# Decoder layer, cross-attention output: stored as half-precision pairs and brought back by transposing DMAs, with one copy less in the running maximum

## Chip, cores, metric

One Trainium2 chip, one core. The metric is device microseconds of one execution; lower is better. TensorE is called PE here, VectorE DVE, ScalarE ACT, GpSimd POOL, and SP is the engine whose queue issues all DMAs of this kernel.

## What is computed

One post-norm decoder layer over 16 sequences of 112 tokens (1792 tokens, width 256): grouped self-attention, then cross-attention, then a feed-forward network with ternary weights, each followed by `layernorm(x + f(x))`. The part that takes most of the time is the cross-attention. All 1792 queries attend to all 16 x 375 = 6000 context rows, in 8 heads of 128:

```
qh, kh, vh = split_heads(x @ Wq), split_heads(ctx @ Wk), split_heads(ctx @ Wv)   # [8, 1792|6000, 128]
sim  = (qh @ kh.T) * 128**-0.5
mean = sim.mean(-1);  sim = (sim - mean) * 1.5 + mean        # a shift per query, which softmax ignores
out  = softmax(sim) @ vh                                      # [8, 1792, 128] -> [1792, 1024]
y    = out @ Wout + bout                                      # [1792, 256]
x    = layernorm(x + y)
x    = layernorm(x + gelu(x @ T(W1).T + b1) @ T(W2).T + b2)   # T: ternary
```

All products keep single-precision accuracy by splitting each operand into a high and a low half-precision part (`f16`) and adding three of the four products.

## The kernel before

**Stages.** Self-attention takes the first 190 us or so. Cross-attention follows, and then a tail with output projection, second layernorm, feed-forward network and third layernorm.

**Cross-attention.** The work is 56 blocks: head h (8) by block of 256 queries (7), `n = 7 h + qb`. The 6016 padded keys of a block are 12 groups of 4 tiles of 128 keys (the last group has 3 tiles). A group is numbered `f = 12 n + s`, 672 in all. At step (n, s) each engine does, in an order written out by hand, a piece of several groups at once:

- PE computes the scores of group f+17 (`scores`, 12 matmuls of 128x256 into a pair of PSUM banks that alternate with f), then `attend(f)`: exponentials, high and low, times the values, added up over the block in bank 4 or 5. Between them lies a `side` task, one that prepares keys, values or queries of a later block. At s = 8 comes `spread`, which writes the row maxima of the next block over all partitions into bank 6.
- ACT copies the scores of group f+17 out of PSUM to a ring of 16 slots in single precision (`keep_scores`, line 847). It waits there until POOL has done with the group that held the slot. It computes the exponentials of group f+3 (`exp_half` for even groups, `exp_full`, lines 854 and 862).
- DVE takes the running maximum of group f+17 straight from PSUM into `run_max` (f16): for the first group of a block a plain copy (line 1081), for the other eleven a maximum with what is in `run_max` (line 1084). PE's `scores` may overwrite a pair of banks when that has been done. DVE also subtracts the maximum from group f+4 (line 1105). At s = 6 it folds the block's maximum (`fold_max`, line 1091). SP transposes the folded maximum with a DMA (`turn`, line 1691), and at s = 8 DVE reduces it (`rows_max`, line 1098); `spread` and the first subtraction of the next block wait for that.
- POOL casts the exponentials of odd groups to f16 (line 1622) and computes the low parts of all groups (line 1628) up to group 658 (`LATE`); after that the low parts of odd groups are DVE's (`low_weights`, line 1124).

**The output of a block.** At s = 1 of the following block DVE inverts the two sums (`invert_sums`) and ACT writes both query tiles, scaled, as single-precision numbers into `o_buf` (`store_output`, 128x128 each). At s = 2 DVE adds a remaining product to the first one (`add_low`, line 1117), and SP stores `o_buf` to DRAM (`store`, line 1680).

**Output projection.** The 1792 rows are 14 tiles of 128 tokens. For each tile SP loads [128 tokens x 1024] in single precision (`load_tile`, 512 KB, line 1699) into one of 5 buffers. PE transposes it in 8 matmuls of 128x128 into banks 0 and 1 (`o_transposes`, line 673). ACT copies the high part out (`o_high`, line 966), DVE computes the low part (`o_low`, line 1311), and PE projects it with 24 matmuls of 128x256 (`o_project`, line 693). Tiles 0 to 4 are transposed at steps TAIL, TAIL+3, ... (TAIL = 657 is step 9 of block 54). Tiles 0 to 3 are projected three steps later each, in three portions after `attend`, the others after the last block, between the pieces of the feed-forward network (`up`, `down`) and its transposes (`n_transposes`).

**SP's queue** is one list in order. What matters near the end is this (block 53 is h = 7, qb = 4):

```
store(53)                       # waits for add_low of block 53, which DVE does in block 54
load_tile(0), (1), (2)
turn(55)                        # the folded maximum of the last block, made at s = 6 of block 54
load of res2                    # the residual stream, 1792 KB
load_tile(3), (4), (5)          # after POOL is through group 657
store(54); load_tile(6) .. (9)
store(55); load_tile(10) .. (13)
```

A `load_tile` waits until the stores of its rows have landed and until its buffer is free.

Of the kernel before, what the change touches and what calls it, by code (L numbers as in the profile page):

```python
# [5 lines left out]
F32 = mybir.dt.float32  # L6
F16 = mybir.dt.float16
ALU = mybir.AluOpType
# [63 lines left out]
def build(nc, xT, x, WA, Wo, ctxT, Wq, Wk, Wv, Wout, bout, W1T, b1, W2T, b2, o_dram, out):  # L72


    with ExitStack() as top:
# [7 lines left out]
        def sem(name):  # L83
# [39 lines left out]
        raw = [at(o, f"raw{r}", [P, NH, DH], F32)  # L123
               for r, o in enumerate((VREG, VREG + 4096, WREG, RING, RING + 4096))]
# [3 lines left out]
        t_dram = nc.dram_tensor("t_scratch", (4, P, W12), F16, kind="Internal").ap()  # L128

        res = at(RING + 12 * 4096, "res", [T, NB, D], F32)  # L130
        res2 = at(KREG, "res2", [P, NT // P, D], F32)
        o_part = o_dram[:, 0:INNER]
# [101 lines left out]
        def batch_tokens(b, n=T):  # L234
# [20 lines left out]
        o_buf = at(SMALL + 32, "o_buf", [P, QT, DH], F32)  # L255
# [10 lines left out]
        (s_qk, s_kept, s_max, s_sub, s_hi, s_exp, s_cast, s_lo, s_av, s_fold, s_bc, s_den, s_oev, s_olo, s_od,  # L266
         s_init) = [
            sem("b_" + n) for n in ("qk", "kept", "max", "sub", "hi", "exp", "cast", "lo", "av", "fold",
                                    "bc", "den", "oev", "olo", "od", "init")]
# [9 lines left out]
        def cols_of(s):  # L279
            return tiles_of(s) * QB  # L280

# [58 lines left out]

        TAIL = NF_ALL - 15
        O_TURN = {3 * i: i for i in range(5)}
        BIASED = {6 + 2 * i: i for i in range(5)}
        O_PROJECT = {3 * i + 3 + x: (i, range(*w)) for i in range(4) for x, w in enumerate(((0, 3), (3, 6), (6, 8)))}
# [9 lines left out]
        oT_hi = [at(KREG + 14336 + 2048 * r, f"oT_hi{r}", [P, NH, P], F16) for r in range(2)]  # L354
        oT_lo = [at(KREG + 18432 + 2048 * r, f"oT_lo{r}", [P, NH, P], F16) for r in range(2)]
# [12 lines left out]
        def bank_of_projection(p):  # L368
            return (7, 3, 2)[p] if p < 3 else 6

        def bank_of_output(p):
            return 6 if p == 5 else 7
# [21 lines left out]
        def columns(c):  # L394
# [7 lines left out]
        (t_bias, t_tr, t_hi, t_lo, t_wp, t_n, t_cp, t_n3, t_add, t_nt, t_yh, t_yl, t_f1, t_ge, t_hh, t_hl, t_f2, t_add2,  # L402
         t_bn, t_bn2, t_ag, t_sq, t_ag3, t_sq3, t_shift,
         t_n3a, t_last, t_out) = [
            sem("t_" + n) for n in ("bias", "tr", "hi", "lo", "wp", "n", "cp", "n3", "add", "nt", "yh", "yl", "f1", "ge",
# [3 lines left out]
        with nc.Block() as block:  # L409

            @block.tensor
            def _(pe):
                def scores(f, more, more_sides, s, qpar):

                    if f >= 2:
                        pe.wait_ge(s_max, more + (f - 1))
# [247 lines left out]
                def o_transposes(i):  # L664
                    pe.wait_ge(s_raw[i % NRAW], 16 * (i // NRAW + 1))
                    if i:
                        pe.wait_ge(t_lo, i)
                    else:

                        pe.wait_ge(s_max, NF_ALL)  # L670
                        pe.wait_ge(s_ident2, 2)
                    for h in range(NH):
                        mm = pe.transpose(psum[:, h // 4, (h % 4) * P:(h % 4 + 1) * P], raw[i % NRAW][:, h, :],
                                          ident2[:, :])
                    mm.then_inc(t_tr, 1)

                def o_project(i, heads=range(NH)):
                    p = i // 2
                    if heads[0] == 0:
                        pe.wait_ge(t_lo, i + 1)  # L680
                        if i == 0:

                            pe.wait_ge(s_free, len(SIDES))
                            pe.wait_ge(s_late, 48)
                        elif i == 6:

                            pe.wait_ge(s_sub, NF_ALL)
                        elif i % 2 == 0 and p >= 4:

                            pe.wait_ge(t_add, p)  # L690
                    for h in heads:
                        for n, (o, w) in enumerate(((oT_hi, wout_hi), (oT_hi, wout_lo), (oT_lo, wout_hi))):
                            mm = pe.matmul(psum[:, bank_of_projection(p), (i % 2) * D:(i % 2 + 1) * D],  # L693
                                           lhsT=o[i % 2][:, h, :], rhs=w[:, h, :],
# [1090 lines left out]
```

## Time and profile before

| | |
|---|---|
| median of 3 runs | 2296.75 us (2296.54 to 2297.69) |
| the profiled execution's own time | 2296.72 us |
| its span in the trace | 2294.9 us |
| busy: PE / DVE / ACT / POOL | 2239.2 / 1972.6 / 1862.2 / 1897.7 us |
| granted clock of PE, mean | 0.998 |
| chain that ended last | PE 83%, POOL 6%, DVE 5%, ACT 2%, issue 2%, DMA 1% |

The span is the stretch between the first and the last recorded instruction; 1.82 us of the execution's time lie around it. Busy times are sums over an engine's instructions; PE's matmuls overlap, so its share says that it was never without one, not that it ran at its peak. Times in the views are microseconds from the start of the span. An entry such as "[1.61 <-DMA ...]" says that the engine stood idle for 1.61 us before the instruction, and what ended that.

### The profile page before, as it was taken

The numbers are of one execution on the slowest core, as the hardware profiler recorded it, in microseconds if no ns is written. First come the engines' busy times: TensorE is split into PE (matmuls) and PEld (weight loads), VectorE is DVE, ScalarE is ACT, GpSimd is POOL, SyncE is SP. The second block draws the span as 40 slices with busy tenths as digits, with TensorE's granted clock in tenths as the row PEclk, the third lists the DMA queues.
The fourth block names the chain that finished last, engine by engine and source line by source line (L and its number), as shares of the span: only waits on it lengthen the run. The fifth ranks groups of instructions, "written<-read, shape, count | busy, mean of one in ns | idle before, by whom it ended". The sixth has DMA issues, their size and how long they took to land.

```text
span 2294.9 us, 61829 instructions
## 1 busy us (share of the span) xinstructions
PE 2239.2 (98%) x25966; PEld 1972.6 (86%) x25966; DVE 1972.6 (86%) x2185; ACT 1862.2 (81%) x2224; POOL 1897.7 (83%) x1155
## 2 busy tenths in 40 slices
PE   7998999999999999999999999999999999999898
PEld 4557998899889998899888998899889988989886
DVE  7888888888888888888888888888888888888877
ACT  4457888888888888888878888888888888888855
POOL 8675888888888888888888898888888888899853
PEclk9999999999999999999999999999999999999999
DMA  6400000000000000000000000000000000011220
GB/s 200 159 32 26 9 9 15 9 11 9 16 9 9 11 8 16 9 9 11 15 9 9 9 9 15 11 9 9 15 9 11 7 11 9 9 24 36 96 79 33
DMA packets 65302, 57.77 MB, mean 25 GB/s; under 512 B 32769, under 2 KB 57857, under 8 KB 65025
## 3 DMA queue, kind: packets, MB, share of 16 engines
q1 hardware_dynamic: 65024, 53.81, 8.5%
q8 instruction: 207, 3.39, 0.6%
q14 instruction: 71, 0.57, 0.1%
HBM read 30.99 MB, written 15.47 MB: 20 GB/s over the span
## 4 chain that ended last, share of the span: by engine, by line
PE 83%; POOL 6%; DVE 5%; issue 2%; ACT 2%; DMA 1%; POOLq 0%; DVEq 0%; ACTq 0%
PE psum L426 32%; PE psum L458 11%; PE psum L451 11%; PE psum L456 6%; PE psum L454 6%; POOL e_lo L1628 5%; PE psum L573 4%; PE psum L563 4%; DVE run_max L1084 2%; PE psum L693 2%; PE psum L580 1%; POOL e_hi L1622 1%; DMA fold_t<-fold 1%; ACT ring L847 1%; PE psum L741 1%
## 5 line engine op out<-in xcount | busy, mean ns | idle before, releaser
L1628 POOL TENSOR_TENSOR e_lo<-ring,e_hi 128x1024 f16<-128x1024 f32 (+1 forms) x665 | 1387.5, 2101 | 195.1 <-ACT ring L862 165.1
L1084 DVE TENSOR_TENSOR run_max<-psum,run_max 128x1024 f16<-128x1024 f32 (+1 forms) x616 | 738.7, 1199 | 180.3 <-ACT ring L847 175.7
L847 ACT ACTIVATE ring<-psum 128x1024 f32<-128x1024 f32 (+1 forms) x672 | 673.7, 1003 | 169.0 <-PE psum L426 91.2
L1105 DVE SCALAR_TENSOR_TENSOR ring<-ring,psum 128x1024 f32<-128x1024 f32 (+1 forms) x672 | 793.8, 1188 | 0.4 <-PE psum L659 0.4
L426 PE MATMUL psum<-qx_hi,k_hi 128*128 128x256 f16 x2632 | 717.5, 273 | 7.8 <-DVE run_max L1084 7.8
L426 PE MATMUL psum<-qx_hi,k_lo 128*128 128x256 f16 x2632 | 717.3, 273 | 0.0
L426 PE MATMUL psum<-qx_lo,k_hi 128*128 128x256 f16 x2632 | 717.3, 273 | 0.0
L458 PE MATMUL psum<-v_main,e_lo 128*128 128x129 f16 x4032 | 710.8, 219 | 0.0
L862 ACT ACTIVATE ring<-ring 128x1024 f32<-128x1024 f32 (+1 forms) x672 | 696.3, 1037 | 0.9 <-DVE ring L1105 0.4
L451 PE MATMUL psum<-v_main,e_hi 128*128 128x257 f16 x2016 | 550.0, 273 | 3.0 <-POOL e_lo L1628 3.0
L456 PE MATMUL psum<-v_main,e_hi 128*128 128x128 f16 x2016 | 446.7, 222 | 0.0
L454 PE MATMUL psum<-v_main,e_hi 128*128 128x129 f16 x2016 | 445.5, 221 | 0.0
L854 ACT ACTIVATE e_hi<-ring 128x1024 f16<-128x1024 f32 x336 | 353.7, 1053 | 101.6 <-DVE ring L1105 101.6
L1622 POOL CAST e_hi<-ring 128x1024 f16<-128x1024 f32 x336 | 341.0, 1015 | 104.0 <-ACT ring L862 101.5
L458 PEld LDWEIGHTS psum<-v_main,e_lo 128*128 128x128 f16 x4032 | 395.5, 98 | 6.9
L426 PEld LDWEIGHTS psum<-qx_hi,k_hi 128*128 128x128 f16 x2632 | 256.8, 98 | 37.7 <-DVE run_max L1084 8.1
L426 PEld LDWEIGHTS psum<-qx_hi,k_lo 128*128 128x128 f16 x2632 | 257.4, 98 | 30.1
L426 PEld LDWEIGHTS psum<-qx_lo,k_hi 128*128 128x128 f16 x2632 | 257.4, 98 | 28.0
L454 PEld LDWEIGHTS psum<-v_main,e_hi 128*128 128x128 f16 x2016 | 197.3, 98 | 25.1
L458 PE MATMUL psum<-v_tail,e_lo 128*128 128x129 f16 (+1 forms) x1232 | 217.9, 219 | 0.0
L451 PEld LDWEIGHTS psum<-v_main,e_hi 128*128 128x128 f16 x2016 | 194.0, 96 | 10.4 <-POOL e_lo L1628 1.9
L456 PEld LDWEIGHTS psum<-v_main,e_hi 128*128 128x128 f16 x2016 | 197.6, 98 | 0.0
(202 smaller groups left out, 3090.2 us busy)
## 6 DMA issues: line engine op xcount, KB each, us to landing
o_scratch<-o_buf SPq DMA_DIRECT2D x56, 128.0 KB, 1.9
raw<-o_scratch SPq DMA_DIRECT2D x14, 512.0 KB, 4.4
stage<-in_ctxT SPq DMA_DIRECT2D x6, 500.0 KB, 4.1
stage<-in_ctxT SPq DMA_DIRECT2D x12, 250.0 KB, 4.9
w_scratch<-wall SPq DMA_DIRECT2D x1, 2304.0 KB, 11.0
wall<-w_scratch SPq DMA_DIRECT2D x6, 384.0 KB, 3.2
x<-in_xT SPq DMA_DIRECT2D x4, 448.0 KB, 6.1
res<-in_x SPq DMA_DIRECT2D x1, 1792.0 KB, 15.4
```

What stands on the lines that cost most here:

```text
L426: mm = pe.matmul(psum[:, 2 * (f % 2) + i // 2, (i % 2) * QB:(i % 2 + 1) * QB], lhsT=k[:, keys], rhs=q[:, qpar, :], start=(n == 0), stop=(n ...
L451: pe.matmul(psum[:, 4 + n % 2, 0:VW], lhsT=e_hi_f[keys, cols], rhs=v_f[keys, i, :], start=(s == 0 and i == 0), stop=False)
L454: pe.matmul(out_t, lhsT=e_hi_f[keys, cols], rhs=v_f[keys, i, 0:OW], start=False, stop=False)
L456: pe.matmul(out_t[:, 0:DH], lhsT=e_hi_f[keys, cols], rhs=v_f[keys, i, OW:VW], start=False, stop=False)
L458: mm = pe.matmul(out_t, lhsT=e_lo_f[keys, cols], rhs=v_f[keys, i, 0:OW], start=False, stop=last_tile and t == QT - 1)
L847: a.activation(ring[:, f % SLOTS, 0:n], pair(f)[:, 0:n], ACT.Copy).then_inc(s_kept, 1)
L854: a.activation(e_hi[f % NEH][:, 0:n], ring[:, f % SLOTS, 0:n], ACT.Exp, scale=SIM_SCALE).then_inc(s_hi, 1)
L862: a.activation(slot, slot, ACT.Exp, scale=SIM_SCALE).then_inc(s_exp, 1)
L1084: ins = v.tensor_tensor(run_max[:, 0:n], pair(f)[:, 0:n], run_max[:, 0:n], ALU.max)
L1105: v.scalar_tensor_tensor(slot, slot, LIFT, psum[:, 6, 0:QB].unsqueeze(1).broadcast_to([P, t, QB]), ALU.add, ALU.subtract).then_inc(s_sub, 1)
L1622: g.tensor_copy(e_hi[f % NEH][:, 0:n], slot).then_inc(s_cast, 1)
L1628: g.tensor_tensor(e_lo[f % NEL][:, 0:n], slot, e_hi[f % NEH][:, 0:n], ALU.subtract).then_inc(s_lo, 1)
```

## The change

Three things change.

1. The running maximum of a block's first group is not taken any more. The second group's maximum reads its own scores from PSUM and the first group's from the ring, in single precision. The copy of line 1081 goes; PE's wait before the scores that overwrite the first group's banks is now for ACT's copy to the ring.
2. The output leaves PSUM as f16 pairs. ACT writes the first query tile in single precision to `o_first` and the second tile's high part straight to `o_buf`. At s = 2 DVE adds the remaining product to `o_first`, computes the second tile's low part from PSUM, and casts `o_first` to its high part (`first_high`). At s = 3 it computes the first tile's low part (`first_low`). The store moves behind that, to s = 3. It has the same number of bytes, in another DRAM tensor whose row holds high and low part of each head. `fold_max` has one more wait, for the low part two blocks back.
3. `load_tile` becomes a transposing DMA [128 tokens x 2048] to [128, 8 heads, 2 parts, 128 tokens] of f16, 512 KB as before. There are 7 buffers. PE's transposes, `o_high` and `o_low` go, for all 14 tiles. Tile i of the first five is projected at steps TAIL+3i to TAIL+3i+2, so that five tiles instead of four are projected beside the last blocks, each from the step at which it was transposed before. After the last block each projection stands one place further ahead in PE's list. The projections rotate over other banks, and the first two `first_residual` of DVE run at TAIL+9 and TAIL+14.

```diff
 def scores(f, past, more_sides, s, qpar):
-    if f >= 2:
-        pe.wait_ge(s_max, more + (f - 1))
+    if f >= 2 and (f - 2) % NGRP == 0:
+        pe.wait_ge(s_kept, past * NQB * NGRP + (f - 1))
+    elif f >= 2:
+        pe.wait_ge(s_max, past * NQB * (NGRP - 1) + maxima_before(f - 2))
...
-            if s == 0:
-                ins = v.tensor_copy(run_max[:, :], pair(f))
-            else:
-                ins = v.tensor_tensor(run_max[:, 0:n], pair(f)[:, 0:n], run_max[:, 0:n], ALU.max)
+            if s == 1:
+                before = ring[:, (f - 1) % SLOTS, :]
+            else:
+                before = run_max[:, 0:n]
+            v.tensor_tensor(run_max[:, 0:n], pair(f)[:, 0:n], before, ALU.max).then_inc(s_max, 1)
...
 def store_output(n):
-    for t in range(QT):
-        a.activation(o_buf[:, t, :], psum[:, 4 + n % 2, O_AT[t]:O_AT[t] + DH], ACT.Copy,
+    for t, dst in enumerate((o_first[:, :], o_buf[:, 1, 0, :])):
+        a.activation(dst, psum[:, 4 + n % 2, O_AT[t]:O_AT[t] + DH], ACT.Copy,
                      scale=o_den[:, t:t + 1]).then_inc(s_oev, 1)
...
 def add_low(n):
     v.wait_ge(s_oev, n * QT + QT)
-    v.scalar_tensor_tensor(o_buf[:, 0, :], psum[:, 4 + n % 2, OW:VW], o_den[:, 0:1], o_buf[:, 0, :],
-                           ALU.mult, ALU.add).then_inc(s_olo, 1)
+    v.scalar_tensor_tensor(o_first[:, :], bank[:, OW:VW], o_den[:, 0:1], o_first[:, :],
+                           ALU.mult, ALU.add).then_inc(s_whole, 1)
+    v.scalar_tensor_tensor(o_buf[:, 1, 1, :], bank[:, O_AT[1]:O_AT[1] + DH], o_den[:, 1:2],
+                           o_buf[:, 1, 0, :], ALU.mult, ALU.subtract).then_inc(s_whole, 1)
+
+def first_high(n):
+    v.wait_ge(s_whole, 2 * n + 1)
+    v.tensor_copy(o_buf[:, 0, 0, :], o_first[:, :]).then_inc(s_ohi, 1)
+
+def first_low(n):
+    v.wait_ge(s_ohi, n + 1)
+    v.wait_ge(s_whole, 2 * n + 2)
+    v.tensor_tensor(o_buf[:, 0, 1, :], o_first[:, :], o_buf[:, 0, 0, :], ALU.subtract).then_inc(s_olo, 1)
...
-O_TURN = {3 * i: i for i in range(5)}
-O_PROJECT = {3 * i + 3 + x: (i, range(*w)) for i in range(4) for x, w in enumerate(((0, 3), (3, 6), (6, 8)))}
+O_PROJECT = {3 * i + x: (i, range(*w)) for i in range(5) for x, w in enumerate(((0, 3), (3, 6), (6, 8)))}
+RESIDUAL = {9: 0, 14: 1}
...
 def o_project(i, heads=range(NH)):
     if heads[0] == 0:
-        pe.wait_ge(t_lo, i + 1)
+        pe.wait_ge(s_raw[i % NRAW], 16 * (i // NRAW + 1))
...
-                   lhsT=o[i % 2][:, h, :], rhs=w[:, h, :],
+                   lhsT=raw[i % NRAW][:, h, o, :], rhs=w[:, h, :],
...
 # PE's list after the last block, without the removed o_transposes
-    o_project(4); n_transposes(0); o_project(5); n_transposes(1); o_project(6)
-    c=0: up, o_project(7), up, (8), down(0), n_transposes(2), (9), down(1), n_transposes(3), (10)
-    c=1: up, (11), up, (12), down(2), n_transposes(4), (13), down(3) in two halves with n_transposes(5) between
+    o_project(5); n_transposes(0); o_project(6); n_transposes(1); o_project(7)
+    c=0: up, o_project(8), up, (9), down(0), n_transposes(2), (10), down(1), n_transposes(3), (11)
+    c=1: up, (12), up, (13), down(2), n_transposes(4), down(3) in two halves with n_transposes(5) between
...
 def load_tile(i):
     sp.wait_ge(s_od, (NBLK - NQB + i // QT + 1) * 16)
     if i >= NRAW:
-        sp.wait_ge(t_tr, i - NRAW + 1)
-    sp.dma_start(raw[i % NRAW][:, :, :].rearrange("p h d -> p (h d)"),
-                 o_part[i * P:(i + 1) * P, :]).then_inc(s_raw[i % NRAW], 16)
+        sp.wait_ge(t_wp, i - NRAW + 1)
+    sp.dma_start_transpose(raw[i % NRAW][:, :, :, :].rearrange("p h x t -> p (h x) t"),
+                           halves_dram[i * P:(i + 1) * P, :]).then_inc(s_raw[i % NRAW], 16)
```

## Rows read from the trace of the kernel before

**Rows 1.** Windows: stretch, length, each engine's busy time, granted clock, DMA share, GB/s.
```profile
265.00:2000.00 1735.00, 1722.99 (x20454) 1563.10 (x20452) 1511.49 (x1559) 1490.10 (x1750) 1489.79 (x865) 1.00 0.05 10
2000.00:2171.00 171.00, 161.53 (x1929) 148.61 (x1927) 149.28 (x147) 147.21 (x167) 156.89 (x94) 1.00 0.16 46
2171.00:2201.00 30.00, 29.98 (x364) 28.33 (x365) 24.70 (x25) 18.77 (x22) 25.67 (x22) 1.00 0.33 110
2201.00:2266.20 65.20, 65.01 (x530) 52.63 (x529) 48.14 (x102) 35.26 (x52) 22.35 (x30) 1.00 0.13 43
```

**Rows 2.** Waits of PE, 265 to 2000: total, times, longest.
```profile
PE psum L659 <- DVE row_max L1098: 6.2, 10, 1.2
```

**Rows 3.** Instructions by tile: ns min/median/max, first and last start.
```profile
L673 PE MATMUL psum<-ident,raw x112: 272/273/303, 2166.1 to 2252.7; 128*128 128x128 f32 x112
...
L966 ACT ACTIVATE oT_hi<-psum x14: 999/1023/1027, 2168.6 to 2253.0; 128x1024 f16<-128x1024 f32 x14
L1311 DVE TENSOR_TENSOR oT_lo<-psum,oT_hi x14: 1210/1218/1226, 2169.6 to 2254.6; 128x1024 f16<-128x1024 f32 x14
...
L1081 DVE CAST run_max<-psum x56: 1210/1224/1226, 158.2 to 2128.6; 128x1024 f16<-128x1024 f32 x56
```

**Rows 4.** The chain that ended last, stretch 2150 to 2295: start, us, what.
```profile
2173.52 0.87 PE psum L673 x8
...
2201.98 2.62 PE psum L693 x24
...
2262.23 0.70 DVE res L1319
...
2263.75 0.26 DVE mean L1328 x2
...
2265.48 0.61 DVE yT_lo L1348
```

**Rows 5.** Waits of PE, 2160 to 2201.
```profile
PE psum L451 <- POOL e_lo L1628: 2.6, 2, 1.4
PE psum L659 <- DVE row_max L1098: 1.9, 1, 1.9
```

**Rows 6.** Timeline of SP's queue: start, us, instruction.
```profile
2150.31 0.36 SPq L1680 DMA_DIRECT2D o_scratch<-o_buf  x1
2150.77 2.40 SPq L1699 DMA_DIRECT2D raw<-o_scratch  x3
2161.41 1.20 SPq L1691 DMA_TRANSPOSE fold_t<-fold  x1
```

**Rows 7.** Timeline of DVE at the last folded maximum.
```profile
2163.86 0.69 DVE L1098 TENSOR_REDUCE row_max<-fold_t 128x2 f16<-128x512 f16 x1 [1.61 <-DMA fold_t<-fold]
```

**Rows 8.** DMA issues of the page: KB each, median us to landing.
```profile
fold_t<-fold SPq DMA_TRANSPOSE x56, 2.4
```

**Rows 9.** Windows over one transposing DMA of 128 KB, issued at 1235.58.
```profile
1236.50:1237.00 0.50, 0.50 (x11) 0.47 (x8) 0.00 (x0) 0.50 (x1) 0.47 (x1) 1.00 0.43 86
1237.00:1237.50 0.50, 0.50 (x11) 0.49 (x10) 0.12 (x1) 0.50 (x2) 0.50 (x1) 1.00 0.88 176
```

**Rows 10.** Timelines of DVE and POOL around 1196, and all folds by line.
```profile
1196.31 1.30 DVE L1091 TENSOR_TENSOR fold<-run_max 128x512 f16<-128x512 f16 x1
...
1196.29 1.04 POOL L1622 CAST e_hi<-ring 128x1024 f16<-128x1024 f32 x1 [0.61 <-ACT ring L862]
...
L1091 DVE TENSOR_TENSOR fold<-run_max x56: 415/419/1301, 189.7 to 2160.3; 128x512 f16<-128x512 f16 x56
```

**Rows 11.** Timelines of DVE, POOL and ACT in a block of the last head.
```profile
2049.39 0.34 DVE L1117 SCALAR_TENSOR_TENSOR o_buf<-psum,o_den,o_buf 128x128 f32<-128x128 f32 x1
...
2052.19 1.21 DVE L1105 SCALAR_TENSOR_TENSOR ring<-ring,psum 128x1024 f32<-128x1024 f32 x1
...
2050.34 4.24 POOL L1628 TENSOR_TENSOR e_lo<-ring,e_hi 128x1024 f16<-128x1024 f32 x2
...
2054.43 1.05 ACT L854 ACTIVATE e_hi<-ring 128x1024 f16<-128x1024 f32 x1
```

More of the change, by code:

```diff
@@ L121, in build @@
         wpack = [wall[:, i, :, :] for i in range(2)]
-        raw = [at(o, f"raw{r}", [P, NH, DH], F32)
-               for r, o in enumerate((VREG, VREG + 4096, WREG, RING, RING + 4096))]
+        raw = [at(o, f"raw{r}", [P, NH, 2, P], F16)
+               for r, o in enumerate((VREG, VREG + 4096, WREG, RING, RING + 4096, KREG + 14336, KREG + 18432))]
         NRAW = len(raw)
@@ L754, in step @@
                     if target < NBLK:
-                        scores(n * NGRP + ahead, past * NQB * NGRP, past * HEAD_SIDES, ts, target % 2)
+                        scores(n * NGRP + ahead, past, past * HEAD_SIDES, ts, target % 2)
                     task = side_of(n, s)
@@ L1024, in _ @@
                         roots(3)
-                    if f - TAIL in O_TURN:
-                        o_high(O_TURN[f - TAIL])
                 store_output(NBLK - 1)
@@ L1401, in last_norms, with first_residual @@
                                         ALU.subtract, ALU.mult).then_inc(t_last, 1)
+                def first_residual(p):
+                    of = res2[:, 2 * p:2 * p + 2, :]
+                    v.wait_ge(t_bias, 2 * p + 2)
+                    v.wait_ge(t_wp, 2 * p + 2)
+                    v.scalar_tensor_tensor(of, psum[:, bank_of_projection(p), :].rearrange("p (i d) -> p i d", i=2),
+                                           1 / WSCALE, of, ALU.mult, ALU.add).then_inc(t_add, 1)
+                    v.wait_ge(t_add, p + 1)
+                    for i in (2 * p, 2 * p + 1):
+                        v.bn_stats(bn2[:, i, :], res2[:, i, :]).then_inc(t_bn, 1)
                 self_attention()
@@ L1422, in _ @@
                         low_half(n, s, halves)
-                    if f + LEAD < NF_ALL:
+                    if f + LEAD < NF_ALL and (f + LEAD) % NGRP:
                         running_max(f + LEAD)
@@ L1431, in _ @@
                         add_low(n - 1)
+                        first_high(n - 1)
+                    if s == 3 and n > 0:
+                        first_low(n - 1)
                     if s == MAX_S and n + 1 < NBLK:
@@ L1440, in _ @@
                             inverse(3)
-                    if f - TAIL - 1 in O_TURN:
-                        o_low(O_TURN[f - TAIL - 1])
-                first_residual(0)
+                    if f - TAIL in RESIDUAL:
+                        first_residual(RESIDUAL[f - TAIL])
                 invert_sums(NBLK - 1)
-                first_residual(1)
                 add_low(NBLK - 1)
+                first_high(NBLK - 1)
+                first_low(NBLK - 1)
                 second_statistics(0)
-                o_low(5)
                 second_norms(0)
-                o_low(6)
                 n_low(0)
                 first_residual(2)
-                o_low(7)
                 n_low(1)
                 hidden_low(0, range(0, 4))
-                o_low(8)
                 first_residual(3)
@@ L1474, in _ @@
                 hidden_low(1, range(4, 8))
-                o_low(13)
                 second_norms(2)
```

120 lines of the change are left out of this document (37 added, 83 removed).

## The prediction

> **What bounds the kernel.** I read the windows first. From 265 to 2000 PE is busy for 1723.0 of 1735.0 us at full clock [rows 1], and what it waits for there is small: 6.2 us for the row maxima [rows 2]. DVE is busy for 87% of that stretch. So an instruction taken off DVE, ACT or POOL there gives time back only where PE waits for it. From 2000 on, in the last head, PE has few side tasks. POOL is busy for 156.9 of 171 us, and PE stands for 9.5 us [rows 1]. From 2171 to 2266 PE is full again: 29.98 of 30.00, then 65.01 of 65.20 [rows 1]. That last stretch is where the change has something to take. The chain of waits agrees: after 2171 it is PE's matmuls, with eight transposes of 0.87 us for each output tile among them, until two dependent chains of small operations near the end [rows 4]. Just before 2171 PE waits 1.9 us for the row maxima of the last block and 2.6 us for low parts from POOL [rows 5]. The row maxima came that late because DVE waited 1.61 us for the transposing DMA of the last folded maximum [rows 7].
>
> **Transposes on PE (gain).** There are 14 x 8 of them [rows 3]. 8 take 0.87 us, 0.109 each at PE's pace [rows 4]. Those of tile 0, at 2166, lie in front of an idle stretch of PE and cost nothing. The other 13 lie on the full stretch: 13 x 0.87 = 11.3 us. ACT's `o_high` (14 x 1.02) and DVE's `o_low` (14 x 1.22) [rows 3] run beside that, and I cost their removal at nothing. PE stays the bound there: two steps take it about 2 x 2.33 = 4.7 us (1.35 for `attend`, 0.98 for nine matmuls of a projection), and POOL's cast, low part and bias, 1.04 [rows 10], 2.12 [rows 11] and 0.7, make 3.9.
>
> **Tile 0's projection (gain).** Its 24 matmuls take 2.62 us [rows 4]. They start three steps earlier, at 2166, where PE has the 0.87 of the transposes and 1.4 of waiting for POOL [rows 5], 2.3 in all. If the row maxima come later still (below), all 2.6 is hidden. I take 2.6.
>
> **New waits of PE (loss).** With less between them, two dependent chains show. After the last `attend`, PE has 0.66 + 2.62 us of projections before `n_transposes(0)`. That needs the normalised tiles 0 and 1, behind: the reciprocal 0.2, ACT's two copies 0.7, two DVE operations of 0.34 [rows 11], the new cast and subtraction at some 0.2 each (a third to a half of that row's size, an estimate), and statistics to norms, which took 1.7 at the end (2263.75 to the low part) [rows 4]. With hand-overs that is about 4.1. So PE waits 0.8. The second is before `up(2)`. It needs `n_low(5)`, in DVE's list behind `first_residual(6)`, 3.9 us of chain (2262.23 to 2266.09) [rows 4]. The 24 matmuls of tile 13 stood between and now stand ahead of `down(2)`. From the end of `down(2)` PE has 40 matmuls, 4.4 us, and DVE's chain is 2.3 (transposes, residual, low part of pair 4) + 3.9 = 6.2. It waited some 0.2 before: 1.6 more. Together 2.4.
>
> **The loads (loss).** This is the term I know least. `turn(55)` stands in SP's queue behind loads 0 to 2. Before, these were issued in 2.40 us from 2150.77, long before 2161.41, when the folded maximum was ready [rows 6]. Now the store of block 53 comes one step later (`first_low` at s = 3), so loads start at about 2153.6, 7.8 us ahead of `turn(55)`. Let r be the time per transposing load, for issue or for transfer, whichever is longer. The last row maxima are then late by D = 3r - 7.8, if positive. The wait for them is on the path already [rows 5, 7], and POOL, ACT and PE follow at once, so D is lost in full. For r the trace shows no such load, but one of a quarter of the size from SBUF: SP is held for 1.20 us [rows 6], the DMA engines are busy for some 0.65 us (0.43 and 0.88 of two half microseconds) [rows 9], the landing takes 2.4 [rows 8]. Lower bound: four times the busy time, r = 2.6, D = 0. Upper bound: four times the landing, r = 9.6, D = 21. Nearest is SP's time, as it is issue that blocks the queue. A plain load holds SP for 0.3 to 0.8; if that much of 1.20 is fixed and the rest goes with size, r = 3.6, D = 3.0. I take 3.0. Loads 3 to 13 have room: with r up to 6 each lands before its projection.
>
> A rule of the Trainium skill speaks for the lower bound: "Advanced Engine Details and Errata", section X-Bar Transpose (TRN2), says that transposing DMAs are as fast as regular ones, 350 to 400 GB/s. By that a load is 1.5 us and D is 0. The windows show 86 and 176 GB/s for the small one [rows 9], so I don't rest on it. Another speaks against the change: "VectorE: DVE Perf Modes", section The three transpose paths, gives 1.3 us for one 128x128 block by DMA and 0.39 by TensorE; 16 blocks would be 21 us a load and the sum a loss. Four blocks landed in 2.4 us here [rows 8], so that figure doesn't simply add up.
>
> **Running maximum (nothing).** The copy, 56 x 1.22 us [rows 3], goes from DVE. It stood at s = 7, between the fold and the row maxima. Where PE waits for those, DVE was waiting for the DMA at the time [rows 7], so the copy hid in that wait. Lower bound of the price 0, best case the 6.2 us [rows 2]. The reading of the ring in single precision beside PSUM I cost like the copy's 1.22, as both rates go by PSUM.
>
> **Output in halves (loss, small).** Each block gets three more DVE operations: 0.34, and twice about 0.2. In sum that is less than the copy that goes, but they stand elsewhere, at s = 2 and 3. Two read SBUF alone, and such an operation waits for POOL: the fold, 0.42 at the median, took 1.30 when POOL's cast began 0.02 us before it [rows 10]. In the last head POOL works without a gap from 2050.34 to 2054.58 [rows 11]. `first_low` would come at about 2052.7, just where the second of the two instructions has begun, and would wait up to 2.0. The subtraction that ended at 2053.40 would then end near 2056.1 instead, and ACT, which needed it at 2054.43 [rows 11], would be 1.7 late, POOL 1.2. POOL is the bound there: 1.2 x 6 blocks = 7.2 us. Had it come 0.1 us earlier, it would slip in between the two and cost POOL 0.2, or 1.2 us. I take 2.0 in all, nearer to the small end, since DVE's phase to POOL is not fixed. In the heads before, POOL has 14% of slack and PE two groups of it: nothing. Store and `fold_max`'s new wait: a store at s = 3 is long done by s = 6.
>
> **Sum.** 11.3 + 2.6 - 2.4 - 3.0 - 2.0 = 6.5 us less. The profiled execution took 2296.72 us against a median of 2296.75, so 2290.2 us. A change of 0.2%, 4.6 us, is about what a measurement of this kernel can tell from none.
>
> **Rivals.**
> A. The forecast, D about 3 and DVE's waits small: 2287 to 2292. Chance 0.34.
> B. Loads are issued as cheaply as plain ones and transfer within 2.6 us. For it: the busy time [rows 9]. Then D = 0, tile 0 hides 2.3, and with 1 to 2 us at POOL the time is 2285.0 to 2287; with nothing lost at POOL and a part of the 6.2 us back, 2283. Chance 0.22.
> C. DVE's small operations meet POOL in the last head (7.2 in place of 2.0: gain 1.3), or r is 5 to 7 (D = 7.2 to 13.2, against 9.5 for all other terms). The time is then 2292 to 2301, most likely 2295.4: no change. For it: rows 11. Chance 0.25.
> D. Slower: transposing loads take 7.3 us or more. The other terms gain 9.5, so r = 5.8 (D = 9.5) cancels the gain, r = 7.3 (D = 14.1) makes the kernel 4.6 slower, and r = 9.6 (D = 21) gives 2296.75 - 9.5 + 21 = 2308.3. For it: landing times, if quarters don't overlap [rows 8]. Against: engine time of 0.65 [rows 9]. Chance 0.12.
> E. Slower: DVE, late by up to 2.3 us at s = 3, makes PE wait for `run_max` in all heads. PE's margin there is two groups minus DVE's own time, about 2. At 0.3 us a block it costs 49 x 0.3 = 15 us: 2305. Against: deterministic phases with gaps of POOL at other places. Chance 0.07.
>
> **Range and chances.** Faster 0.56 (A, B), same 0.25 (C), slower 0.19 (D, E). 2283.5 to 2300 leaves out some 2 in 10, nearly all above; A and B alone span 2283 to 2292.
>
> **What would show it.** In the new profile: no L673 group; PE full from 2171 to the end of `down(3)`, with 0.8 before the first `n_transposes` and 1.8 before `up(2)`; SP's rows for `raw` at about 3.6 us each, and `turn(55)` some 3 us after its fold. DVE's `first_low` group at 0.2 us or far above it tells A from C, POOL's gaps in the last head too. The prediction is wrong if r is far from 3.6, or if PE's waits from 265 to 2000 grow past 12 us.

## The result and the profile after

The changed kernel takes 2344.89 us (median of 5 runs, 2341.26 to 2354.69) against 2296.75: ratio 1.0212, 95% interval 1.0199 to 1.0225. It is slower by 2.1%, outside the range of the prediction and in the other direction. The profiled execution took 2354.69 us with a span of 2352.9, so the rows below come from one that is some 10 us above the median.

The windows of the changed kernel, against [rows 1]; the last three stand in the tail and are taken up further down: stretch, length, busy time of PE, weight loads, DVE, ACT, POOL, granted clock, DMA share, GB/s.

```profile
265.00:2000.00 1735.00, 1680.42 (x19823) 1519.04 (x19821) 1551.17 (x1606) 1446.29 (x1699) 1448.15 (x839) 1.00 0.04 10
2223.60:2228.50 4.90, 0.17 (x4) 0.00 (x0) 1.40 (x2) 1.03 (x2) 4.68 (x3) 0.95 0.93 166
2228.50:2230.00 1.50, 1.46 (x12) 1.33 (x13) 1.03 (x1) 0.00 (x0) 0.00 (x0) 0.50 0.99 345
2230.00:2231.50 1.50, 1.50 (x15) 1.34 (x13) 1.50 (x3) 1.06 (x1) 0.00 (x0) 0.52 1.07 371
```

PE now lacks 54.6 of 1735 us; before it lacked 12.0. So the time is lost in the heads, where the prediction had said "nothing". The waits of PE, first for 265 to 2000 (against [rows 2]), then for the whole run:

```profile
PE psum L670 <- DVE row_max L1075: 42.7, 28, 2.2
PE psum L437 <- DVE run_max L1059: 11.8, 8, 2.4
...
PE psum L670 <- DVE row_max L1075: 54.5, 36, 4.8
PE psum L437 <- DVE run_max L1059: 21.2, 16, 2.4
```

Over the whole run the same two waits were before:

```profile
PE psum L659 <- DVE row_max L1098: 13.5, 16, 2.0
PE psum L426 <- DVE run_max L1084: 7.8, 7, 2.5
```

They grew by 41.0 and 13.4, together 54.4 us. From the last `spread` to the end the changed kernel is 5.9 us shorter (124.4 against 130.3), so ahead of it 58.0 + 5.9 = 63.9 us were lost: 54.4 in these waits, 2.3 ahead of the first scores (157.8 in place of 155.5), and some 7 that the waits do not hold. The granted clock fits these 7. Before, it stayed at full speed from 55 to 2294 us; in the profiled execution of the changed kernel it fell to 0.50 four times ahead of the last `spread`, near 197, 1013, 1245 and 1535 us, for 3.4 us each. One of the four, and the kernel before over the whole stretch:

```profile
1013.00:1016.00 3.00, 3.00 (x24) 2.62 (x22) 2.10 (x3) 2.30 (x3) 0.00 (x0) 0.50 0.00 0
```

```profile
55.00:2294.00 2239.00, 2198.30 (x25672) 1950.34 (x25668) 1930.47 (x2126) 1837.93 (x2185) 1849.17 (x1115) 1.00 0.08 21
```

Each can have cost PE 1.4 us, by the matmuls of the two windows at the end of the last section, or 1.7, half of 3.4. Four are 5.6 to 6.8 us (an estimate). The loss is spread over the heads: in each of the first seven, from one head's first `spread` to that of the next, the changed kernel takes 258 to 263 us, against 251 to 255. The chain that ended last also changed its nature. Before it was 83% PE; now its first line is

```profile
PE 47%; POOL 19%; DVE 16%; issue 10%; ACT 5%; DMA 3%; SPq 0%; POOLq 0%; DVEq 0%; ACTq 0%
```

Which instruction makes DVE late? DVE's groups from 265 to 2000 in the changed kernel: busy us, mean ns, idle before.

```profile
L1108 DVE TENSOR_TENSOR o_buf<-o_first,o_buf 128x128 f16<-128x128 f32 x46 | 94.7, 2059 | 0.0
L1068 DVE TENSOR_TENSOR fold<-run_max 128x512 f16<-128x512 f16 x46 | 66.8, 1453 | 0.7
L1075 DVE TENSOR_REDUCE row_max<-fold_t 128x2 f16<-128x512 f16 x47 | 32.2, 686 | 82.3 <-DMA fold_t<-fold 82.3
L1103 DVE CAST o_buf<-o_first 128x128 f16<-128x128 f32 x47 | 18.1, 385 | 0.0
L1098 DVE SCALAR_TENSOR_TENSOR o_buf<-psum,o_den,o_buf 128x128 f16<-128x128 f32 x47 | 16.1, 343 | 0.0
```

`first_low` (L1108), a subtraction of 128x128, takes 2.06 us in the mean, where the prediction had "some 0.2". The fold went from a mean of 0.68 us to 1.45. The 82.3 us idle in front of `row_max` look like a cause and are none: most of it is the place that the copy of the running maximum left (the first experiment has 89.7 there and loses nothing). One block in the timelines of DVE and POOL, and PE's waits from 1060 to 1090:

```profile
1068.08 0.33 DVE L1103 CAST o_buf<-o_first 128x128 f16<-128x128 f32 x1
1068.33 1.21 DVE L1082 SCALAR_TENSOR_TENSOR ring<-ring,psum 128x1024 f32<-128x1024 f32 x1
1069.45 1.21 DVE L1059 TENSOR_TENSOR run_max<-psum,run_max 128x1024 f16<-128x1024 f32 x1
1070.59 2.19 DVE L1108 TENSOR_TENSOR o_buf<-o_first,o_buf 128x128 f16<-128x128 f32 x1
1072.70 1.21 DVE L1082 SCALAR_TENSOR_TENSOR ring<-ring,psum 128x1024 f32<-128x1024 f32 x1
...
1080.42 2.32 DVE L1068 TENSOR_TENSOR fold<-run_max 128x512 f16<-128x512 f16 x1
...
1068.40 4.23 POOL L1607 TENSOR_TENSOR e_lo<-ring,e_hi 128x1024 f16<-128x1024 f32 x2
...
1080.33 4.41 POOL L1607 TENSOR_TENSOR e_lo<-ring,e_hi 128x1024 f16<-128x1024 f32 x2
```

```profile
PE psum L670 <- DVE row_max L1075: 1.8, 1, 1.8
```

Each of these POOL rows is two subtractions of 2.1 us, both reading SBUF alone. The first ends near 1070.5. `first_low` comes at 1070.59, just after the second has begun, and ends with it, 1.9 us later than it would without POOL (in experiment 5 such an operation takes 0.28 us where it meets nothing). This is what the prediction drew for the last head at 2052.7. It happens in every one of the 46 blocks from 265 to 2000: the minimum is 1.71 us and the median 2.19. The delay moves DVE against POOL for the rest of the block. The fold, 0.42 us at 1050.22 in the same block before, now comes 0.09 us after a pair has begun and takes 2.32. The row maxima are late by that, and PE waits 1.8 us for them. Other blocks pass without a wait or wait for `run_max`: 36 waits of 1.5 us in the mean from 265 to 2000.

The Trainium skill states as a rule what the prediction had taken from [rows 10]: "SBUF — State Buffer", section SBUF: two separate sides, has a port pair that DVE and GpSimd share as an exclusive lock; a DVE operation with two SBUF inputs takes it against a GpSimd operation that reads SBUF, and the one that comes second waits for the whole instruction of the other. The rows above agree, and so do experiments 2 to 6.

### The profile page after: what moved, and what is told of

It reads as the page before. It is cut to its first block, busy times and chain, and to the rows that moved or that the text cites. A ratio compares the mean times of both kernels' runs of the same rounds, so it can differ in the third digit from the quotient of the medians.

```text
span 2352.9 us, 61943 instructions
## 1 busy us (share of the span) xinstructions
PE 2245.5 (95%) x25854; PEld 1968.4 (84%) x25854; DVE 2057.8 (87%) x2283; ACT 1849.8 (79%) x2210; POOL 1904.4 (81%) x1155
## 4 chain that ended last, share of the span: by engine, by line
PE 47%; POOL 19%; DVE 16%; issue 10%; ACT 5%; DMA 3%; SPq 0%; POOLq 0%; DVEq 0%; ACTq 0%
PE psum L437 17%; POOL e_lo L1607 15%; DVE run_max L1059 6%; PE psum L469 5%; PE psum L462 5%; POOL e_hi L1601 4%; PE psum L574 4%; DVE ring L1082 3%; DMA fold_t<-fold 3%; PE psum L467 3%; PE psum L465 3%; PE psum L584 2%; ACT ring L838 2%; DVE fold L1068 2%; ACT ring L853 1%
## 5 line engine op out<-in xcount | busy, mean ns | idle before, releaser
L1059 DVE TENSOR_TENSOR run_max<-psum,run_max 128x1024 f16<-128x1024 f32 (+1 forms) x560 | 667.6, 1192 | 103.3 <-ACT ring L838 102.6
L437 PEld LDWEIGHTS psum<-qx_hi,k_lo 128*128 128x128 f16 x2632 | 257.8, 98 | 30.5
## 6 DMA issues: line engine op xcount, KB each, us to landing
w_scratch<-wall SPq DMA_DIRECT2D x1, 2304.0 KB, 11.3
```

The source lines that it names most:

```text
L437: mm = pe.matmul(psum[:, 2 * (f % 2) + i // 2, (i % 2) * QB:(i % 2 + 1) * QB], lhsT=k[:, keys], rhs=q[:, qpar, :], start=(n == 0), stop=(n ...
L1059: v.tensor_tensor(run_max[:, 0:n], pair(f)[:, 0:n], before, ALU.max).then_inc(s_max, 1)
```

## Experiments

Each kernel was timed beside the kernel before on the same chip; ratios are against that.

**1. The running maximum alone, on the kernel before.**

```
 running_max(f) at s = 1:  max(pair(f), ring[f - 1]) -> run_max     (no copy at s = 0)
 the waits of scores on s_max become maxima_before(...), as in the change
```

> The kernel before with the first part of the change alone: no copy for a block's first group, the second group's maximum reads the first one's scores from the ring in single precision. Port theory (DVE operations with both inputs in SBUF wait until POOL's running instruction ends; this maximum has one input in PSUM): 2294 to 2299 us, mean of the new maximum 1.22 us, PE's waits for the row maxima below 15 us. Rival M (the changed maximum or PE's changed wait makes DVE late): over 2310 us.

Measured: 2298.06 us, ratio 0.9997 (0.9987 to 1.0007). The new maximum takes 1.22 us, PE waits 3.8 us for row maxima. This part neither costs nor gives.

**2. The changed kernel with the first tile's sum in PSUM.** The arithmetic, the number and the order of instructions are those of the change; only the place of the sum differs, which one instruction writes and two read.

```
-  scalar_tensor_tensor(o_first, bank[:, OW:VW], o_den[:, 0:1], o_first, mult, add)
+  scalar_tensor_tensor(o_sum, bank[:, OW:VW], o_den[:, 0:1], o_first, mult, add)   # o_sum = psum[:, 6, 256:384]
-  tensor_copy(o_buf[:, 0, 0, :], o_first);  tensor_tensor(o_buf[:, 0, 1, :], o_first, o_buf[:, 0, 0, :], subtract)
+  tensor_copy(o_buf[:, 0, 0, :], o_sum);    tensor_tensor(o_buf[:, 0, 1, :], o_sum, o_buf[:, 0, 0, :], subtract)
```

> The kernel after, with one thing moved: add_low writes the first tile's sum to free columns of PSUM bank 6 in place of SBUF, so that the cast and the subtraction (first_high, first_low) read one input from PSUM. Same operations, sizes and order. Port theory: first_low falls from 2.06 us to about 0.2 to 0.35, the fold back to a mean of 0.7, blocks to their periods of before (252.8 us a head), and the tail keeps its gain of about 6 us: 2287 to 2293 us. Rival R (three more DVE operations and a later store make DVE late whatever they read): over 2330 us.

Measured: 2290.50 us (2286.39 to 2291.78, 6 runs), ratio 0.9961 (0.9948 to 0.9974). DVE's groups and PE's wait, 265 to 2000:

```profile
L1109 DVE TENSOR_TENSOR o_buf<-psum,o_buf 128x128 f16<-128x128 f32 x48 | 13.6, 284 | 0.0
L1069 DVE TENSOR_TENSOR fold<-run_max 128x512 f16<-128x512 f16 x48 | 32.6, 678 | 0.7
```

```profile
PE psum L671 <- DVE row_max L1076: 5.4, 12, 1.5
```

Against the changed kernel some 54 us go away, and the gain of the tail stays. The later store and the new wait of `fold_max` are in this kernel too, so they are not what cost the time.

**3 and 4. One more DVE operation at s = 3 of the kernel before**, 128x128, once with two SBUF operands, once with one of them in PSUM. `fold_max` waits for it two blocks back, as it does for `first_low` in the change.

```
+  if s == 3 and n > 0:
+      tensor_tensor(fold[:, 384:512], A, fold[:, 256:384], subtract)
       # 3: A = fold[:, 0:256] read as 128 f32        4: A = psum[:, 6, 0:128]
```

> The kernel before with one more DVE operation per block at s = 3: a subtraction 128x128 of two inputs in SBUF, whose result nothing uses. Port theory: it takes about 2 us on average in place of 0.2, DVE comes late to the fold, and the time is 2315 to 2350 us. Rival R (it needs the number of operations and the later store): 2296 to 2300 us.

> The same extra subtraction at the same place, but with its first input from PSUM. Both theories: 0.2 to 0.3 us each, 2296 to 2300 us. If it is over 2310 us, an extra operation at s = 3 costs by its place and not by where it reads.

Measured: 2298.50 us, ratio 0.9999 (0.9989 to 1.0008), and 2296.76, ratio 0.9994 (0.9984 to 1.0004). The fourth is as expected. The third is a miss: the SBUF operation cost nothing. Its rows say why, again DVE and then POOL:

```profile
1007.57 0.43 DVE L1098 TENSOR_TENSOR fold<-fold 128x128 f16<-128x128 f32 x1
...
1005.72 4.29 POOL L1636 TENSOR_TENSOR e_lo<-ring,e_hi 128x1024 f16<-128x1024 f32 x2
```

It comes 1.85 us after POOL's pair began, not 2.19 as `first_low` does at 1070.59. POOL's first instruction is still running. The operation waits for its end, gets the port before the second, and all of this takes 0.43 us. Its group from 265 to 2000:

```profile
L1098 DVE TENSOR_TENSOR fold<-fold 128x128 f16<-128x128 f32 x48 | 45.1, 940 | 0.0
```

Over the 48 the median is 0.43 us and the mean 0.94; so most slip in and a minority waits: 33 take about 0.43 us, and the 15 others, which arrive 2.15 or 2.45 us after the pair's start, 2.04 us or more. The operands alone do not explain the loss. The time of arrival would have to, and in the changed kernel that is set by the two small operations which it adds ahead, at s = 2. That became the next theory.

**5 and 6. The same two kernels with two small copies from PSUM at s = 2**, 0.29 us each, which do nothing but move the arrival.

```
   if s == 2 and n > 0:
       add_low(n - 1)
+      for i in range(2): tensor_copy(fold[:, 384:512], psum[:, 6, 0:128])
```

> The kernel before with the added 128x128 subtraction of two SBUF operands at s = 3 (as in the run with that alone, which cost nothing) and, new, two small PSUM-reading copies behind add_low at s = 2, 0.28 us each, as the changed kernel has second half and high half there. They are there only to let the subtraction arrive later: it came 1.85 us after the start of POOL's pair of SBUF instructions of 2.1 us each, and should now come some 2.2 to 2.4 after. Phase theory: it comes just after POOL's second instruction has begun, waits for its end, takes about 2 us in most blocks (mean above 1.7), the fold and the row maxima are late as in the changed kernel, and the time is 2320 to 2350 us. Rival (it is the amount of DVE's work, or another place of the change, that does it): a mean near 1 us and no change, 2297 to 2300, since 1.5 us a block more of DVE work did nothing before.

> The same kernel as the one beside it, the two small copies at s = 2 too, but the added subtraction at s = 3 takes its first operand from PSUM. Phase theory and shared-port theory together: an operation with a PSUM operand does not meet POOL, takes 0.28 us wherever it falls, and the time is that of before, 2296 to 2300 us. If three more operations on DVE were too many by themselves, it would be slower by the same 30 to 50 us as its neighbour.

Measured: 2336.63 us, ratio 1.0176 (1.0159 to 1.0193), and 2297.49, ratio 1.0001 (0.9991 to 1.0010). Both as the theory said. The operation of the fifth in the block at 1026:

```profile
1026.06 2.17 DVE L1104 TENSOR_TENSOR fold<-fold 128x128 f16<-128x128 f32 x1
...
1023.85 4.23 POOL L1643 TENSOR_TENSOR e_lo<-ring,e_hi 128x1024 f16<-128x1024 f32 x2
```

and its group, and that of the sixth, 265 to 2000:

```profile
L1104 DVE TENSOR_TENSOR fold<-fold 128x128 f16<-128x128 f32 x47 | 84.0, 1787 | 0.0
```

```profile
L1104 DVE TENSOR_TENSOR fold<-psum,fold 128x128 f16<-128x128 f32 x48 | 13.5, 281 | 0.0
```

It now comes 2.21 us after the start of the pair, 0.36 us later than in the third kernel, and the run takes nearly 40 us more. The sixth has the same three operations more and loses nothing, so it is not the amount of work. The fifth kernel shows the mechanism without the rest of the change, but not the whole size: the sum in SBUF costs some 54 us (experiment 2). In 7 of the 47 blocks the operation of the fifth arrives at 2.1 us and slips in with 0.28 us, which `first_low` never does.

**7. The changed kernel, `first_low` at s = 4 in place of s = 3.**

> The changed kernel with one line moved: first_low, both operands in SBUF still, runs at s = 4 instead of s = 3, behind running_max. There it should arrive some 4.5 us after the start of POOL's pair, when both of POOL's instructions (4.2 us) are over and its next cast is 0.8 us away. Phase theory: mean below 0.8 us instead of 2.06, fold near 0.68, and the time falls from 2344.9 to about 2289 to 2294 (the store leaves a step later, so the first loads of the last head start about 1 us later than with the sum in PSUM). Rival (an SBUF,SBUF operation costs 2 us in every place, or DVE has too much work): 2335 to 2350.

Measured: 2327.44 us, ratio 1.0133 (1.0116 to 1.0150). The place matters, by some 17 us, but the size was missed. At s = 4 the operation meets POOL's cast or a pair as well: 0.88 us at the least, a median of 0.96, up to 2.27. With both operands in SBUF I have found no place in the block that is free in every head. Its group, and what PE waited for, 265 to 2000:

```profile
L1108 DVE TENSOR_TENSOR o_buf<-o_first,o_buf 128x128 f16<-128x128 f32 x47 | 58.7, 1250 | 0.0
```

```profile
PE psum L437 <- DVE qx_lo L1045: 18.6, 14, 1.5
PE psum L670 <- DVE row_max L1075: 18.1, 25, 2.1
```

Put together (means in us, 265 to 2000; the last column is the median against the kernel before beside it; for the changed kernel the first comparison):

| kernel | the operation | fold | PE's wait for `row_max` | time |
|---|---|---|---|---|
| 4, PSUM | 0.28 | 0.68 | 4.7 | -1.7 |
| 6, PSUM, later | 0.28 | 0.68 | 5.7 | +0.5 |
| 3, SBUF | 0.94 | 0.62 | 4.1 | +0.1 |
| 7, SBUF at s = 4 | 1.25 | 1.08 | 18.1 | +30.5 |
| 5, SBUF, later | 1.79 | 1.35 | 37.5 | +39.7 |
| changed | 2.06 | 1.45 | 42.7 | +48.1 |

A mean of 0.94 us is absorbed. In the kernels from 1.25 on the fold is hit as well, and PE pays.

**8. Sum in PSUM, and `turn(55)` behind two loads, not three.**

```
-  for i in range(3): load_tile(i)
-  turn(NBLK - 1)
+  load_tile(0); load_tile(1); turn(NBLK - 1); load_tile(2)
```

> The kernel with the sum in PSUM and one change in SP's queue: turn(55) is issued behind two of the three first loads of the last head, not behind all three. With the sum in PSUM the three loads held SP from 2154.29 to 2162.63, the last folded maximum was ready at 2161.97, turn(55) went at 2162.73, landed after 3.3 us, and PE stood for 3.51 us before the last spread. Theory (the loads delay turn(55) by issue and by transfers in flight): two loads hold SP to about 2159.7, turn(55) goes as soon as the fold ends, lands in 2.4 to 3.3 us, PE's stand shrinks from 3.5 to 2.0 to 2.8, and the time is 0.7 to 1.5 us less than with the sum in PSUM alone: 2289 to 2290 where that is 2290.5. Rival (the landing is long for another reason, so that the place in the queue hardly matters): PE's stand stays above 3.2 and the time at 2290.5.

Measured: 2291.33 us, ratio 0.9965 (0.9952 to 0.9979): no gain over experiment 2. PE's stand before the last `spread` did shrink, from 3.51 to 1.96 us. But SP reached the load of `res` later (2166.93, in experiment 2 2163.99), and from the last `spread` to the last `attend`'s end it takes 1.3 us longer than there. The same edit in experiment 10 shows what is late next.

**9. Sum in PSUM, and PE's last part in another order**, to test the new waits: `o_project(6)` and `(7)` ahead of `n_transposes(0)` and `(1)`, `o_project(13)` behind `n_transposes(4)`. `o_project(6)` also waits for the last `first_low`.

> The kernel with the sum in PSUM, PE's order of the last part changed at two places: o_project(6) in front of n_transposes(0) and o_project(7) in front of n_transposes(1), and o_project(13) behind n_transposes(4), as in the kernel before. It tests the term called new waits of PE, which measured 2.38 us before n_transposes(0) and 1.20 before up(2). Theory (the waits are chains of other engines that other matmuls can cover): both go to below 0.6 and 0.3; the 24 matmuls of 2.6 us now cover the first, some 1 us may show again before n_transposes(1); 2.0 to 3.2 us less: about 2287.3 to 2288.5. Rival (the chain simply appears behind the next piece): under 1 us gained, 2289.5 to 2290.5.

Measured: 2289.43 us, ratio 0.9959 (0.9945 to 0.9972). The wait of 2.38 us before `n_transposes(0)` and that of 1.20 before `up(2)` are gone; one of 1.42 stands before `up(0)` instead, and two of 1.1 in sum for the low parts that `down` reads (`hT_lo`), where there was one of 0.3. The span is 1.7 us shorter than that of experiment 2, a little under what was expected.

**10. Experiments 8 and 9 together.**

> Sum in PSUM, turn(55) behind two loads, and PE's changed order together. If the two places are independent the gains add: 2.7 to 4.7 us less than with the sum in PSUM alone, 2286 to 2288 us, 10 to 12 us less than before.

Measured: 2290.40 us, ratio 0.9962 (0.9948 to 0.9976); span 2286.7 against 2286.8 for experiment 9. The gains do not add. Timeline of POOL in experiment 10:

```profile
2171.49 1.03 POOL L1606 CAST e_hi<-ring 128x1024 f16<-128x1024 f32 x1
2174.11 0.73 POOL L1491 TENSOR_TENSOR res<-res,bout_b 128x256 f32<-128x256 f32 x1 [1.59 <-DMA res<-o_scratch]
```

The load of `res` went from ahead of a transposing load to behind one, SP issued it 2.6 us later than in experiment 9, and POOL stood 1.59 us for it.

**11 and 12. As 10, with `res` loaded ahead of the third tile; and as 11, with `o_project(7)` split**, five heads ahead of `n_transposes(1)` and three behind.

> The kernel with the sum in PSUM, turn(55) behind two loads and PE's changed order, and one more change in SP's queue: the load of the residual (res) goes ahead of the third load, not behind it. Without it, turn(55) behind two loads took PE's stand from 3.2 to 1.95 us, but the time stayed at about 2290: SP issued the residual's load 2.6 us later (2165.74 in place of 2163.10), POOL stood 1.59 us for it before its first add_bias, and from there to 2197 POOL has no gap, at 4.75 us per two groups. Theory (POOL bounds that stretch, so what counts is when it can start): POOL's stand for res goes, its full stretch ends 1.0 to 1.6 us earlier, at about 2195.2, the last attend as well or until PE's own 4.7 per two groups bounds, and the span is 0.8 to 1.5 us shorter than 2286.7. Rival (PE itself is the bound there and POOL's full row is a coincidence): POOL's stand goes and nothing changes at the end, 2286.4 to 2287.0.

> The same and, in PE's last part, o_project(7) split: five heads of it, 1.64 us, ahead of n_transposes(1) and three behind, so that the chain of normalised tiles (transposes, high part, low part) starts at about 2207.9 in place of 2208.8 and is covered by 1.0 us of matmuls. PE's wait before up(0), 1.42 us, should go to 0.2 to 0.6, and the time fall by 0.8 to 1.2 against its neighbour. If DVE's first_residual(2) in front of n_low(1) is what is late, the wait only shrinks by 0.4 or less. In sum 2287 to 2289 where before is 2298, or 10 to 11 us less than before.

Measured: 2288.12 us, ratio 0.9960 (0.9947 to 0.9974), span 2286.1; and 2287.48, ratio 0.9957 (0.9944 to 0.9971), span 2285.2. POOL's stand is gone, and the span is 0.6 shorter, less than the 0.8 to 1.5 expected. The split took the wait before `up(0)` from 1.41 to 0.43 us and 0.9 off the span, as expected. Experiment 2, experiments 8 to 10, and 11 and 12 ran on three different chips, each group beside the kernel before. By their intervals they can't be told from each other; the order among them rests on spans and rows of single executions. All are faster than before, by 0.35 to 0.43%.

## Why the prediction was wrong, step by step

**Output in halves: the step that failed.** "In the heads before, POOL has 14% of slack and PE two groups of it: nothing." The mechanism was right and stood in the text, the arrival at the second of POOL's two instructions and the wait of up to 2.0 us. I gave it to the last head alone and, for the heads before, put it at nothing because POOL and PE had slack there. It measured 2.06 us in the mean over the 46 blocks from 265 to 2000, and the fold rose by 0.77 as well. Rival E had the place, DVE late by up to 2.3 us in all heads, but put 0.3 us a block on it (measured: 54.4 / 49 = 1.1) and a chance of 0.07. It named PE's wait for `run_max`, which grew by 13.4; three times as much, 41.0, came by the fold and the row maxima, which the step did not follow. Slack as a share of busy time was the wrong measure: an operation that comes second waits for the rest of the other engine's instruction, however much slack there is elsewhere.

The last head, where the step had a price, was mis-sized too. From the `spread` of 2017.32 to the last, 2228.54, the changed kernel takes 211.2 us; with the sum in PSUM it is 203.9 (1962.90 to 2166.79), and before 202.2. So 7.3 us were lost there, 1.3 of them in the longer stand before the last `spread` (4.76 against 3.51) and 6.0 ahead of it, where the sum had 2.0 and rival C 7.2.

"DVE's phase to POOL is not fixed" was wrong too, and the trace of before had the answer. In [rows 11] the `subtract` in whose place `first_low` would stand starts 1.85 us after POOL's pair (2052.19 and 2050.34). In head 3 the same two stand at 1041.53 and 1039.68, a block earlier at 1006.07 and 1004.21: 1.85 and 1.86. The phase is the same to 0.01 us in three blocks of two heads. Over all 55 blocks of the trace of before it is 1.85 or 1.86 us in 39, 2.45 in 14, and something else in two. To it come the new operations ahead, 0.25 to 0.5 us (0.34 measured), and POOL's second instruction begins at 2.1 and ends at 4.2. So a wait of nearly 2 us in most blocks and of some 1.4 in the others could be forecast; that the fold would then meet POOL as well was possible, but not to be read from these rows.

**Running maximum: right.** Experiment 1 lost and gained nothing, and the maximum that reads the ring takes 1.22 us.

**The loads: near in size, by another way.** Timeline of SP, and DVE's row for the last maxima, in the changed kernel (against [rows 6, 7]):

```profile
2216.39 8.01 SPq L1678 DMA_TRANSPOSE raw<-halves_scratch  x3
2224.49 1.21 SPq L1670 DMA_TRANSPOSE fold_t<-fold  x1
...
2227.80 0.69 DVE L1075 TENSOR_REDUCE row_max<-fold_t 128x2 f16<-128x512 f16 x1 [3.48 <-DMA fold_t<-fold]
```

r was 2.7 us a load in front of `turn(55)`, 2.5 in the median, against 3.6. PE's stand before the last `spread` grew from 1.91 to 4.76, 2.85 us against D = 3.0. That the two agree is chance. By the prediction's own formula, 3r - 7.8, the 8.0 us of the three loads give a D of 0.2. What came late was this: DVE's wait for the last folded maximum grew from 1.61 to 3.48, by 1.9 us. Of that, 1.0 is that `turn(55)` was issued 1.0 us after its fold had ended (the loads started 7.1 us ahead of it, not 7.8), and 0.9 that the landing took 3.3 us in place of 2.4 with the loads under way, which D had not counted. The fold itself took 1.00 us, as before in this block (1.04). The other 1.0 us of PE's longer stand is that PE was done sooner after the end of the fold, 0.3 us behind it in place of 1.3. Transposing loads land in 5.4 us (median of 14). The Trainium skill's 1.3 us a block of 128x128 ("VectorE: DVE Perf Modes", section The three transpose paths) would make that 21 if blocks simply added up (an estimate), which these rows refute. The 350 to 400 GB/s of the Trainium skill ("Advanced Engine Details and Errata", section X-Bar Transpose (TRN2)) would make it 1.5 (an estimate) and are not reached by these loads alone either: 237 GB/s stood in the window from 2222.2 to 2223.6.

**Transposes, and tile 0's projection.** With the sum in PSUM the tail can be read without the loss of the heads. From the last `spread` to the end experiment 2 takes 121.7 us against 130.3, 8.6 less, where the terms said 11.3 + 2.6 - 2.4 = 11.5. Behind the last `attend` it is 87.9 against 94.6, 6.7 less: nine tiles' transposes (7.8) and one projection (2.6) less, 3.9 more of waits. Ahead of it only 1.9 of the 3.2 come through (five tiles' transposes, 4.35, and a wait of 1.44 less, one projection more). "PE stays the bound there" no longer quite held. POOL's groups from 2171 to 2198, before and then with the sum in PSUM, and a step of the latter in the timelines:

```profile
L1628 POOL TENSOR_TENSOR e_lo<-ring,e_hi 128x1024 f16<-128x1024 f32 x5 | 12.0, 2404 | 4.3 <-ACT ring L862 4.3
```

```profile
L1608 POOL TENSOR_TENSOR e_lo<-ring,e_hi 128x1024 f16<-128x1024 f32 x6 | 17.7, 2951 | 3.0 <-ACT ring L854 3.0
```

```profile
2174.70 3.12 POOL L1608 TENSOR_TENSOR e_lo<-ring,e_hi 128x1024 f16<-128x1024 f32 x1
...
2174.08 1.74 DVE L1116 TENSOR_TENSOR e_lo<-ring,e_hi 128x1024 f16<-128x1024 f32 x1 [1.49 <-POOL e_hi L1602]
```

The same port, the other way round. In this stretch DVE makes every second `e_lo`, 1.74 us from SBUF. POOL's comes 0.6 us behind it, stands 1.0 us and is recorded with 3.12. I had summed 1.04 + 2.12 + 0.7 = 3.9 for POOL's two steps; it is 4.75 (2174.70 to 2179.45), against PE's 4.7. So what is taken off PE there does not come back in full.

**New waits of PE.** The waits of PE in the tail of the changed kernel:

```profile
PE psum L710 <- DVE norm L1317: 2.4, 1, 2.4
PE psum L722 <- DVE yT_lo L1323: 1.2, 1, 1.2
PE psum L462 <- DVE e_lo L1115: 0.9, 2, 0.5
```

2.4 where I said 0.8, and 1.2 where I said 1.6, and one of 0.35 before the first half of `down(3)`: 3.9 in place of 2.4. The first chain took 5.9 us from the end of the last `attend` (2263.42 to 2269.31), not 4.1; a part that I had no row for stands in it, the load of ACT's table ahead of the square root:

```profile
2266.77 1.28 ACT L956 ACT_TABLE_LOAD   x1 [2.32 <-DVE inv L1305]
2268.06 0.21 ACT L956 ACTIVATE inv<-inv 128x4 f32<-128x4 f32 x1
```

**In sum** the terms of the tail were off by 1.3, 1.5 and less. With the sum in PSUM the change gives 6.4 us between the spans of before and of experiment 2, and 7.9 between the medians side by side (2298.43 and 2290.50), where the forecast was 6.5. That they agree is in part luck: the 6.5 held 2.0 us of waits for POOL that experiment 2 does not have, so the terms that are left said 8.5. And it says nothing for a prediction whose largest term was taken as nothing. The time of rival B, 2285.0 to 2287, does not follow from its own terms either: 11.3 + 2.3 - 2.4 less 1 to 2 at POOL is 9.2 to 10.2, or 2286.5 to 2287.5.

## What to carry to other kernels

Ahead of adding an operation with two SBUF inputs to DVE while POOL works from SBUF, measure in the timeline how long after the start of POOL's instruction it would arrive, in several blocks: here it took two values, 1.85 and 2.45 us, in 53 of 55 blocks, all readable before the change. Price the operation by what is left of that instruction, and follow the delay to the next hand-over (here fold, DMA, row maxima). Or put one operand into PSUM, which here turned 2.06 us into 0.28 at no other cost that the runs show. And in a queue, what stands behind a slow transfer may be wanted sooner than the transfer itself (here `turn(55)`, then `res`).

## What was unexpected in the hardware

- 0.36 us in arrival decide over 1.7 us in one operation and nearly 40 us in the run. Where DVE waits for the first of two POOL instructions it gets in between them; POOL's pair then takes 4.29 in place of 4.23.
- The granted clock fell to 0.50 (1.2 GHz) at PE's stand before the last `spread` in some executions and not in others, and the length of the stand does not sort them. It fell in the changed kernel (stand of 4.76 us; the windows from 2223.60 to 2231.50 above) and in experiments 3, 4, 6, 7 and 9 to 12 (1.91 to 4.88 us). It did not in the kernel before (1.91), nor in experiments 1, 2, 5 and 8 (1.92 to 3.51 us). The kernel before and experiment 6 have the same stand of 1.91 us. Windows behind it, before and then in experiment 6:

```profile
2164.60:2168.00 3.40, 3.40 (x46) 3.30 (x47) 2.98 (x3) 1.45 (x2) 2.74 (x2) 1.00 1.01 331
```

```profile
2165.80:2169.10 3.30, 3.30 (x26) 3.11 (x24) 3.21 (x4) 1.72 (x2) 2.37 (x2) 0.50 1.04 345
```

  The one has 46 matmuls in 3.4 us at full clock, the other 26 in 3.3 us. By that, such a fall costs PE some 1.4 us (an estimate). Experiments 9 to 12 had one at this place and experiment 2 had one at 199 us, so it does not explain what 10 to 12 gained less than expected. What decides over it stays open.
